# A mixture-of-experts kernel: rows gathered in quarters and turned by VectorE in place of TensorE

## The reference

```python
x = x + attn(layernorm(x), w_qkva, gamma)
x = x + ffn(layernorm(x), router_w, w0, w1, wo)

def attn(x, w_qkva, gamma):              # x: (8, 1024, 256)
    h = rmsnorm(x, gamma)
    q, kv, a = split(einsum('bnd,ed->bne', h, w_qkva), 3)
    a = sigmoid(a)
    y = scan(y[n] = a[n] * y[n-1] + kv[n])   # along the 1024 tokens
    return q * y

def ffn(x, router_w, w0, w1, wo):        # G=8 groups, S=1024, M=256, E=8, H=1368
    raw = softmax(einsum('GSM,ME->GSE', x, router_w))
    # top-2 choice; a choice beyond capacity C=256 of an expert and group is dropped
    dispatch, combine = gating_top2(raw, C)  # (G, S, E, C), combine holds the gates
    xin = einsum('GSEC,GSM->EGCM', dispatch, x)
    hid = gelu(einsum('EGCM,EMH->EGCH', xin, w0)) * einsum('EGCM,EMH->EGCH', xin, w1)
    eo  = einsum('EGCH,EHM->EGCM', hid, wo)
    return einsum('EGCM,GSEC->GSM', eo, combine)
```

## Time and profile before

| what | value |
|---|---|
| median of 3 runs | 1694.92 us (1693.82 to 1695.25) |
| span of the profiled execution | 1694.7 us |
| PE busy | 1657.8 us |
| DVE busy | 866.7 us |
| ACT busy | 723.9 us |
| POOL busy | 505.2 us |
| DMA moved | 96.21 MB, 124980 packets |

### The profile page before, as it was taken

One profiled execution on the slowest core, in us unless ns is written; L12 is line 12 of the kernel. 1 busy time (PEld: TensorE's weight loads), 2 busy tenths in 40 slices (PEclk: granted clock), 3 DMA queues, 4 the chain that ended last, 5 costly groups with the idle time before them and its releaser, 6 DMA issues.

```text
span 1694.7 us, 22843 instructions
## 1 busy us (share of the span) xinstructions
PE 1657.8 (98%) x8738; PEld 1435.3 (85%) x8738; DVE 866.7 (51%) x1827; ACT 723.9 (43%) x1325; POOL 505.2 (30%) x432
## 2 busy tenths in 40 slices
PE   8999979899999999999999999999999999999998
PEld 7888868788888888888888888888888888888887
DVE  7998744435544454346444644455445544464442
ACT  5776624234433443335333533344334433353332
POOL 2155556463222222222222222222222222222211
PEclk9999989999999999999999999999999999999999
DMA  7553121025111331124111511151114211241101
GB/s 165 160 157 115 52 77 53 3 43 127 33 26 26 91 61 26 26 53 92 20 26 23 121 21 26 26 118 33 26 26 94 58 26 26 56 90 20 23 11 15
DMA packets 124980, 96.21 MB, mean 57 GB/s; under 512 B 27144, under 2 KB 120776, under 8 KB 124872
## 3 DMA queue, kind: packets, MB, share of 16 engines
q1 hardware_dynamic: 96200, 60.66, 13.2%
q0 software_dynamic: 28672, 34.10, 12.1%
HBM read 60.11 MB, written 34.61 MB: 56 GB/s over the span
## 4 chain that ended last, share of the span: by engine, by line
PE 89%; POOL 3%; DVE 2%; DMA 2%; issue 2%; another core or an unknown queue 1%; ACT 0%; SPq 0%; POOLq 0%; DVEq 0%; ACTq 0%
PE bank L1579 27%; PE bank L1592 27%; PE bank L1608 17%; PE bank L1610 9%; PE bank L1396 4%; POOL slots L592 2%; PE bank L1482 2%; PE bank L1449 1%; DMA slots<-records,sloti 1%; PE bank L1603 1%; PE bank L1605 1%; POOL out L659 1%; PE bank L1437 1%; PE bank L1412 1%
## 5 line engine op out<-in xcount | busy, mean ns | idle before, releaser
L1335 DVE TENSOR_TENSOR y<-bank,sig 128x512 f32<-128x512 f32 (+1 forms) x352 | 243.0, 690 | 472.0 <-PE bank L1592 442.1
L659 POOL DMA_INDIRECT out<-xring,slot_records x128 | 214.7, 1678 | 890.7 <-DVE xring L1315 826.2
L1608 PE MATMUL bank<-wo,hhi 128*128 128x512 f32 (+1 forms) x1276 | 447.2, 388 | 0.0
L844 ACT ACTIVATE hhi<-y 128x512 fp32r<-128x512 f32 (+1 forms) x349 | 220.4, 631 | 524.5 <-DVE y L1335 486.7
L1610 PE MATMUL bank<-wo,hlo 128*128 128x256 f32 (+1 forms) x1396 | 382.0, 274 | 0.0
L1338 DVE TENSOR_TENSOR hlo<-y,hhi 128x512 fp32r<-128x512 f32 (+1 forms) x349 | 241.5, 692 | 243.4 <-ACT hhi L844 237.8
L834 ACT ACTIVATE sig<-bank 128x512 f32<-128x512 f32 (+1 forms) x352 | 208.9, 594 | 284.4 <-PE bank L1579 272.2
L1608 PEld LDWEIGHTS bank<-wo,hhi 128*128 128x128 f32 (+1 forms) x1276 | 239.2, 187 | 43.5
L1610 PEld LDWEIGHTS bank<-wo,hlo 128*128 128x128 f32 (+1 forms) x1396 | 261.7, 187 | 6.5
L1579 PE MATMUL bank<-xThi,whi 128*128 128x512 f32 x704 | 216.1, 388 | 7.0 <-ACT sig L834 5.4
L1592 PE MATMUL bank<-xThi,whi 128*128 128x512 f32 x704 | 213.0, 383 | 0.4 <-DVE y L1335 0.3
(11 more groups left out here) (134 smaller groups left out, 1571.0 us busy)
## 6 DMA issues: line engine op xcount, KB each, us to landing
stage<-in_L_ffn_w_kernel SPq DMA_DIRECT2D x160, 128.0 KB
stage<-in_L_ffn_wo_kernel SPq DMA_DIRECT2D x80, 128.0 KB
xring<-in_L_attn_x SPq DMA_DIRECT2D x16, 512.0 KB
out<-xring SPq DMA_DIRECT2D x16, 512.0 KB
x_rows<-rows SPq DMA_DIRECT2D x16, 512.0 KB
slots<-records,sloti POOLq DMA_INDIRECT x128
rows<-x_rows,slot_records POOLq DMA_INDIRECT x128
out<-xring,slot_records POOLq DMA_INDIRECT x128, 3.8
```

Of the source, the lines that this page charges most:

```text
L659: pool.indirect_dma_start(out_rows, bass.IndirectOffsetOnAxis(idx, 0), ysb[:, t % 2, j, :], None, compute_op=ALU.add).then_inc(added, 16)
L844: act.activation(h_high(e, t, hc)[0:n, :], hf[0:n, hc % 2, :], ACT.Copy).then_inc(h_hi, 1)
L1335: dve.tensor_tensor(hf[0:n, hc % 2, :], up_value(e, t, hc)[0:n, :], gel[0:n, hc % 2, :], ALU.mult).then_inc(mul_done, 1)
L1608: pe.matmul(lines(yb[j][:, :]), high, lines(wo[0:n, hc, :, :].rearrange("p s c -> p (s c)")), start=hc == 0, stop=end, skip_group_check=True)
```

## The change

From the second expert on (tiles 4 to 31) the rows are fetched and turned in another way:
- A record has one gate (of the choice that it belongs to), the token's number, the row's number and four numbers of the row's quarters. `records` is kept apart for the two choices. `gates` and what belonged to it is gone, and the products with the gate read it from `slot_records`.
- `x2_pieces` is the same DRAM array seen as quarters of 64 words. `gather` issues 16 indirect DMAs of 128 quarters (256 B each) a tile, in place of 4 of whole rows. Their order puts the quarters where a transpose of 32x32 blocks leaves them as a matrix of columns by slots.
- SP loads the records once more in another layout for this (`load_pieces`, 4 DMAs of 32 partitions), and `load_records` is 4 DMAs of 32 partitions too.
- `turn_rows` is a DVE transpose of 128x512, after chunks 4 and 6, from SBUF to SBUF (`rowsT`, the room of `xn`). TensorE's `prepare` returns at once for e > 0. ACT and DVE read `rowsT` in place of the PSUM bank.
- The columns come out in the order (p k), and the weights are loaded in that order for e > 0.
- GpSimd sets up the constant fields of the records with 13 more `iota`s.

The diff, cut to its core:

```diff
 def load_records(e, t):
-                sync.dma_start(slot_records[:, t], src.rearrange("o (p j) c -> p (o j) c", p=P)).then_inc(
-                    records_loaded[t], 16)
+                to = slot_records[:, t].rearrange("p j c -> p (j c)")
+                by_token = src.rearrange("o (i b j) c -> b i (o j c)", b=NB, j=FJ)
+                for b in range(NB):
+                    sync.dma_start(to[32 * b:32 * (b + 1), :], by_token[b]).then_inc(records_loaded[t], 16)
+
+            def load_pieces(n):
+
+                e, t, p = n // FT, n % FT, n % 2
+                if n >= FT + 2:
+                    sync.wait_ge(rows_loaded[p], landed_rows(n - 2))
+                at = (e * ESLOTS + t * T) * REC
+                flat = slots.rearrange("s c -> (s c)")
+                for b in range(NB):
+                    src = flat[at + b:at + b + 32 * NP * REC].rearrange("(i w) -> i w", i=32)
+                    sync.dma_start(piece_slots[32 * b:32 * (b + 1), p, 0:NP * REC - NB],
+                                   src[:, 0:NP * REC - NB]).then_inc(pieces_loaded[p], 16)
...
@@ SP, expert
                         load_records(e + 1, t - 1)
+                    if FT <= FT * e + t + 3 < E * FT:
+                        load_pieces(FT * e + t + 3)
                     if t == FT - 1 and not last:
...
@@ GpSimd, gather
                 if n >= 2:
-                    pool.wait_ge(ft, KD * (n - 1))
-                for j in range(FJ):
-                    idx = slot_records[:, t, j, SRC:SRC + 1].bitcast(I32)
...
+                    pool.wait_ge(ft, KD * min(n - 1, FT))
+                if n >= FT + 2:
+                    pool.wait_ge(turned, KD * (n - 1 - FT))
...
+                pool.wait_ge(pieces_loaded[p], 16 * NB * ((n - FT) // 2 + 1))
+                into = rows2[:, p].rearrange("p j c -> p (j c)")
+                for i in range(NP):
+                    b, j = divmod(i, FJ)
+                    idx = piece_slots[:, p, i * REC + PIECE:i * REC + PIECE + 1].bitcast(I32)
+                    to = (j * NB + b) * PW
+                    pool.indirect_dma_start(into[:, to:to + PW], None, x2_pieces[t],
                                             bass.IndirectOffsetOnAxis(idx, 0)).then_inc(rows_loaded[p], 16)
...
@@ VectorE
-                        if hc == PREPARE[0] and t < FT - 1:
-                            gates(e, t + 1)
...
+                        if hc in TURN and FT <= FT * e + t + 1 < E * FT:
+                            turn_rows(*divmod(FT * e + t + 1, FT), TURN.index(hc))
...
+            def turn_rows(e, t, k):
+
+                n, p = FT * e + t, t % 2
+                dve.wait_ge(rows_loaded[p], landed_rows(n))
+                pieces = rows2[:, p].rearrange("p j c -> p (j c)").rearrange("p (n i k) -> p k n i", n=NP, k=KD)
+                dve.transpose(rowsT[:, k, :].rearrange("p (n i) -> p n i", n=NP), pieces[:, k]).then_inc(turned, 1)
...
@@ TensorE, prepare
                 p = t % 2
+                if e > 0:
+                    return
                 if k == 0:
-                    pe.wait_ge(rows_loaded[p], 16 * FJ * (FT // 2 * e + t // 2 + 1))
+                    pe.wait_ge(rows_loaded[p], landed_rows(t))
```

More of the change, by code:

```diff
@@ L97, in build @@
     REC = 8
-    GT1, GT2, EX1, TOK, SRC = range(5)
+    GATE, TOK, ROW, PIECE = range(4)
+    NB = P // 32
+    NP = T // 32
+    PW = D // NB
     ESLOTS = G * CAP
@@ L111, in build @@
     assert (G, KD, TILES, FT, T, FJ) == (8, 2, 8, 4, 512, 4) and E * 16 <= P
+    assert PIECE + NB < REC and NP == NB * FJ and PW == KD * 32
     slots = nc.dram_tensor("slots", [NSLOT + 4 * S, REC], F32, kind="Internal").ap()
     x2_rows = [nc.dram_tensor(f"x2_rows{t}", [2 * S + 1, D], F32, kind="Internal").ap() for t in range(FT)]
+    x2_pieces = [r.rearrange("r (b c) -> (r b) c", b=NB) for r in x2_rows]
     out_rows = out.rearrange("g s c -> (g s) c")
@@ L189, in build @@
         part = sb("part", [P, FJ, D])
[L190 to L192 removed]
+        records = sb("records", [P, 2, 2, TILES, REC])
         slot_records = sb("slot_records", [P, FT, FJ, REC])
@@ L322, in build @@
         fx_lo = sem("fx_lo")
-        gate_done = sem("gate_done")
+        pieces_loaded = [sem(f"pieces_loaded{i}") for i in range(2)]
+        turned = sem("turned")
         part_done = sem("part_done")
@@ L387, in build, with landed_rows @@
         assert HC == 11
+        def landed_rows(n):
+            calls = [FJ if i < FT else NP for i in range(n % 2, n + 1, 2)]
+            return 16 * sum(calls)
         def staged(eng, e, hc):
@@ L539, in _ @@
             pool.memset(ones[:, :], 1.0)
-            pool.memset(records[:, :, :, :], 0.0).then_inc(consts_raw, 1)
+            pool.memset(records[:, :, :, :, :], 0.0).then_inc(consts_raw, 1)
             pool.memset(zero[:, :], 0.0)
@@ L543, in _ @@
             pool.wait_ge(consts_raw, 4)
-            pool.iota(fill[:, :, :, SRC].bitcast(I32), pattern=[[0, 2], [0, FJ]], base=2 * S, channel_multiplier=0)
-            pool.iota(records[:, :, :, SRC].bitcast(I32), pattern=[[S, 2], [P, TILES]], base=0, channel_multiplier=1)
+            pool.iota(fill[:, :, :, ROW].bitcast(I32), pattern=[[0, 2], [0, FJ]], base=2 * S, channel_multiplier=0)
+            for b in range(NB):
+                pool.iota(fill[:, :, :, PIECE + b].bitcast(I32), pattern=[[0, 2], [0, FJ]], base=2 * S * NB + b,
+                          channel_multiplier=0)
+            for r in range(2):
+                for c, m in ((ROW, 1), *((PIECE + b, NB) for b in range(NB))):
+                    pool.iota(records[:, r, :, :, c].bitcast(I32), pattern=[[0, 2], [m * P, TILES]],
+                              base=m * S * r + max(c - PIECE, 0), channel_multiplier=m)
             pool.iota(fill[:, 0, :, TOK].bitcast(I32), pattern=[[1, FJ]], base=NTOK - T, channel_multiplier=FJ)
@@ L749, in prepare @@
             def prepare(e, t, k):
-                act.wait_ge(ft, KD * FT * e + KD * t + k + 1)
-                act.activation(xThi[:, t % 2, k, :], tr[:, :], ACT.Copy).then_inc(fx_hi, 1)
+                if e == 0:
+                    act.wait_ge(ft, KD * t + k + 1)
+                    act.activation(xThi[:, t % 2, k, :], tr[:, :], ACT.Copy).then_inc(fx_hi, 1)
+                else:
+                    act.wait_ge(turned, KD * FT * (e - 1) + KD * t + k + 1)
+                    act.activation(xThi[:, t % 2, k, :], rowsT[:, k, :], ACT.Copy).then_inc(fx_hi, 1)
             def step(i):
@@ L1045, in placing @@
                 row = records[:, g.parity]
-                row_gates = row[:, :, GT1:GT2 + 1].rearrange("p t k -> p k t")
+                row_gates = row[:, :, :, GATE]
                 if n == 0:
```

58 lines of the change are left out of this document (23 added, 35 removed).

## The result

The changed kernel takes 1897.15 us (median of 4 runs, 1892.09 to 1914.65) against 1694.37 us of the kernel before beside it (1691.51 to 1695.25). The ratio is 1.1223, with a 95% interval from 1.1187 to 1.1258. I had said 1695.0 us, and no more than 1705. The profiled execution has a span of 1890.3 us and a mean granted clock of 0.952.

A forecast was written before the change was run, and what follows sets the result against it. TensorE (PE) alone was taken to set the time; 1694.7 - 26.6 (transposes) - 0.5 (gates) + 1.1 (records) + 6.6 (six changes) + 17.0 (first change) + 2.7 (clock) = 1695.0 us, forecast's own range 1689 to 1700, overall 1685 to 1705.

The forecast's parts named there:

- the one on GpSimd: POOL's gathers: twelve more a tile, 15.9 us, free in a steady expert but not once, in the first expert.
- What PE saves: TensorE without its transposes: two groups of four a tile in 28 tiles, 0.475 us each, 26.6 us saved.
- What DVE gets: Two 128x512 transposes a tile on VectorE, 0.7 us each (bounds 0.4 and 1.4), fitting into a fourth-tile gap: price 0.
- What a gather costs: On POOL a quarter gather costs as much as a row gather: 1.03 us and 0.30 us to the next.
- the delay of the adds: POOL, first expert: adds of tile 2 start 14.7 us later behind the extra gathers, delaying the second expert's weights.
- the gap of 17 us: TensorE at the change from first to second expert, near 405 us: 17.0 us idle, plus 2.7 us for a lowered clock.
- What SP gets: Eight small loads ahead of the weights in SP's queue, not one: first chunk 2.5 us later, net 2.0 at seven changes.
- what a late first chunk costs: Six later expert changes: 1.2 us each on TensorE, 7.2 us, less 0.6 lost already: +6.6 us.
- The relief from smaller gathers: Expert changes: gathers beside the first weight chunks move fewer bytes, so the first chunk lands 0.5 us sooner (0 to 1.2).
- The cover: Expert changes: 2.2 us of ACT's wait for first weights are free, through the chunk buffers between ACT and PE.
- the clock behind these small gaps: TensorE's clock at the later expert changes: steady waits of 1.2 us do not lower it, so nothing was charged.
- The slow rival: Quarter gathers keep DMA engines busy while first weight chunks load in fourth tiles: +10.5 us, 1705 us; chance 0.20.

The follow-up runs named there:

- e4: Changed kernel, with GpSimd waiting after each four of a tile's 16 quarter gathers until they have landed: 1713.99 us, ratio 1.0126.
- e2: Changed kernel, but rows gathered as four whole rows a partition (4 DMAs a tile, not 16), VectorE still turning them; output differs: 1705.91 us, ratio 1.0072.
- f1: e4 with SP issuing the next expert's first four weight chunks ahead of the small loads of records and piece numbers: 1680.18 us, ratio 0.9938.
- g1: f1 with the fourth tile's records and piece numbers loaded only after the seventh weight chunk: 1667.42 us, ratio 0.9892.
- g3: Kernel before, plus 12 quarter gathers of 32 partitions a tile from the second expert on, into a buffer nobody reads: 1702.99 us, ratio 1.0101.
- e3: Kernel before, plus 12 quarter gathers of 128 partitions a tile from the second expert on, into a buffer nobody reads: 1950.94 us, ratio 1.1526.

## Why the prediction was wrong

**The step that failed** is the one on GpSimd: "Twelve more a tile are 15.9 us. In a steady expert that is free: POOL has 44 us of work in 180, and its adds wait for the end of the tile anyway." I asked whether POOL had the time, and it had; I did not ask what POOL's work does to others while it runs. Sixteen gathers in an unbroken row hold back TensorE's signals. With the row broken the kernel stands at 1714 us (e4), so this one mechanism is 183 of the 203 us, 6.5 us in each of 28 tiles. The trace of before held a warning that I passed by: `remote` waits of 7.1 and 3.6 us of ACT and DVE, behind a row of twelve indirect DMAs in the drain. I used the gap for its clock and never asked what had made it. Whether it had the same cause is open.

**What PE saves** was right. Steady tiles take 43.9 us in place of 44.9 (the first of an expert 44.3 in place of 45.2) wherever the signals come in time (e2, f1, g1), 0.95 by my rows, and g1 has 28.2 us less PE busy time than the kernel before (26.6 foreseen).

**What DVE gets** was right: 705 ns each, where I had taken 0.7, and hidden in the fourth tile too.

```profile
L1165 DVE STREAM_TRANSPOSE xn<-rows x56: 702/705/707, 418.1 to 1820.2; 128x512 f32<-128x512 f32 x56
```

The estimate from the Trainium skill ("Vector Engine (DVE) Microarchitecture Reference", section 3.8), 0.53 us, was too low by a quarter.

**What a gather costs** was right (996 ns for 1025), and the delay of the adds by 14.7 us was nearly so: in g3, with twelve gathers more and SP as before, ACT waits for the first weights for 14.41 us where it waited for 1.44, so 13.0 longer. In the changed kernel it does not show as the gap of 17 us that I had announced: ACT waits only 5.87 us and PE 3.31 us, and TensorE stands in holes of 3.28 and 4.80 us just before, at 389 and 398, while POOL gathers. Where the holes are gone, it is there in full (20.63 us in e4, whose train takes some 5 us longer by its three rests).

**What SP gets, and what a late first chunk costs**, was sized too low. I had +1.2 us a change. In e4, the changed kernel without the holes, the six later fourth tiles take 46.3 to 48.0 us for 43.9, so 2.4 to 4.1 more, and in e2 48.8. SP's queue at the first change of the changed kernel, against the earlier trace rows:

```profile
406.03 1.69 SPq L503 DMA_DIRECT2D slot_records<-slots  x4
407.76 1.81 SPq L514 DMA_DIRECT2D piece_slots<-slots  x4
409.62 1.74 SPq L385 DMA_DIRECT2D stage<-in_L_ffn_w_kernel  x2
```

The eight small loads keep the queue for 3.6 us, 0.45 each, so 3.2 more than before and not 2.5. The first pair of weight loads takes 1.74 us for 0.94 (the later pairs 1.19), which I had left out, though the diff changes their order of rows. The relief from smaller gathers did come: at the later changes ACT waits 4.5 to 4.8 us with quarters, and 5.3 to 5.7 in e2 with whole rows. But 3.4 us was my figure.

The cover was right, and the step behind it was wrong. ACT's wait for the first weights and TensorE's gap behind it, at the second change of e2:

```profile
581.66 0.63 ACT L876 ACTIVATE whi<-stage 128x512 fp32r<-128x512 f32 x1 [5.51 <-DMA stage<-in_L_ffn_wo_kernel]
...
584.31 1.22 PE L1636 MATMUL bank<-xThi,whi 128*128 128x512 f32 x2 [2.96 <-DVE y L1381]
```

The gap is 2.55 us shorter than the wait, and so it is at every change of e2 and e4 and in g3 (14.41 and 11.86), for a cover of 2.2 in my sum. What I had put at nothing is the clock behind these small gaps ("The steady waits of 1.2 us do not do that"). The gaps were 2.1 us in e4 and 3.0 in e2. Behind e2's the granted clock was 0.50 for the next 2.6 us (403.40 to 406.00), which makes 4.9 us of loss out of 3.0 of standing. Behind e4's six it was 1.00 three times and 0.60 to 0.71 three times, and those are the fourth tiles of 46.3 to 46.5 and of 47.7 to 48.0 us.

Even with the row of gathers broken, the kernel stands 19 us above my sum (1714 for 1695). The six later changes hold 12 of them (19.5 us where I had 7.2), and the first change some 4.

**The slow rival**, contention of the transfers, named the right side and the wrong mechanism, so it was right by luck. The rule of 512 B of the Trainium skill ("DMA: Bandwidth & Descriptors", Specifications), which stood beside it, did not decide: the DMA engines are busy for 0.23 of the time in the slow experts, and for 0.27 with the same quarters in g1, where nothing waits; and the first weights came sooner beside quarters of 256 B than beside whole rows of 1 KB.

The rule that would have pointed the other way, away from the truth, is in the Trainium skill's page "SBUF — State Buffer", in the section "SBUF: two separate sides": the ports of the engines and those of DMA are separate and cannot contend. A reader takes from it that loads which nobody reads can't slow TensorE's chain down. Here they did, by 15% (e3), though by a way that need not be a port of SBUF.

**What stays open** is the path on which a signal of TensorE and the transfers of GpSimd's gathers meet. The traces show the sender done, the receiver waiting, and other senders in time; they don't show what lies between. That the signal is late is read from the records of the matmuls, whose ends are modelled; but the matmuls behind them started on time, and the runs without a profile lose as much. Nor was the count of partitions varied on one and the same chip, or the gathers' source moved. And why one chip of three shows no such wait, in the drain where the others have them, is not known; if I had run the changed kernel there, I could say whether it would be slow at all.

## What to carry over

GpSimd's indirect loads have a price that isn't in GpSimd's own time: a tile may have many of them, but more than some eight of 128 partitions in a row made other engines wait here, though perhaps not on every chip. Break the row after four to eight with something else to do, or with a wait; here 2 us of an engine with time to spare gave back 180. Run two variants on the same chip before comparing what they wait for. And when small loads are added ahead of large ones in a queue, look whether the large ones can go first: that turned a kernel 1.3% slower into one 1.1% faster, with no load less.

## What the hardware showed that I had not expected

- 16 indirect gathers of 128 partitions x 256 B, one each 1.25 us, delay what waits for TensorE by up to 10.8 us from about the ninth on (a few from the sixth), until the row ends. 12 gathers of 32 partitions behind four of 128, at the same rate, delayed nothing, but on a chip that showed no such delay anywhere.
- About 1.7 to 2 us without an issue are enough to be rid of it, whether POOL waits or fills a buffer meanwhile.
- In the same microseconds ScalarE starts 0.04 us after VectorE, VectorE 0.03 us after ScalarE, and TensorE 0.06 us after VectorE.
- TensorE's gap of 3.0 us in e2 was followed by 2.6 us at a granted clock of 0.50; behind gaps of 2.1 us in e4 it was 1.00 three times of six.
- A gather of 32 partitions keeps POOL for 945 ns and one of 128 for 991: the price hangs on the instruction far more than on the count of rows.
- A load of 32 partitions takes SP's queue 0.42 to 0.45 us; one of records over 128 partitions takes 0.32 (0.36 to the start of the next).
